# Masked keys for a cross attention's scores, values laid out for whole-row transfers, and a new order of work

## The reference

```
q, k, v = x @ Wq + bq, ctx @ Wk + bk, ctx @ Wv + bv        # 16 heads of 8
scores  = q . k / sqrt(8)
scores  = 0.5 * (scores * mask) + 0.5 * scores             # mask: 0 or 1
attn    = softmax(clip(scores, -50, 50))
y       = layernorm(x + (attn @ v) @ Wo + bo) * gamma + beta
```

```
q, k, v = rms_norm(y) @ to_qkv_w;  q, k = rope(q), rope(k)
keys    = [memory token x16, persistent x16, causal keys of the own segment]
x1      = y + softmax(q . keys / 8) @ values @ to_out_w
a, g    = rms_norm(x1) @ ff_w1 + ff_b1
out     = x1 + (silu(g) * a) @ ff_w2 + ff_b2
```

## Time and profile before

| | us |
|---|---|
| median of 3 runs | 1323.95 (1317.02 to 1329.44) |
| the profiled execution's own time | 1315.27 |
| its span, first to last instruction | 1313.5 |
| TensorE busy | 1155.9 (88%) |
| TensorE weight loads busy | 1001.2 (76%) |
| ScalarE busy | 1000.9 (76%) |
| GpSimd busy | 997.8 (76%) |
| VectorE busy | 954.3 (73%) |

### The profile page before, as it was taken

How to read it: one execution, slowest core, us unless ns; L and a number is a source line. 1 busy time by engine, 2 the same in 40 slices (tenths; PEclk the granted TensorE clock), 3 DMA queues, 4 the chain that set the end, 5 groups by cost and what they waited for, 6 DMA issues and landing times.

```text
span 1313.5 us, 53289 instructions
## 1 busy us (share of the span) xinstructions
PE 1155.9 (88%) x19811; PEld 1001.2 (76%) x19811; DVE 954.3 (73%) x2511; ACT 1000.9 (76%) x3149; POOL 997.8 (76%) x1678
## 2 busy tenths in 40 slices
PE   0569899999999999999999999999999999999986
PEld 0457788787788878787887878887787878887875
DVE  2446787778777877877787777778778777877772
ACT  1247788888888878788888887888888878888864
POOL 1246788888888888887888888788888888887874
PEclk9978999999999999999999999999999999999999
DMA  6322333333333333334333433333333333334321
GB/s 173 108 82 80 127 120 103 126 124 110 105 129 124 99 121 124 110 109 131 124 108 107 129 122 99 124 124 103 112 125 124 103 122 124 110 108 133 125 78 36
DMA packets 137337, 149.07 MB, mean 113 GB/s; under 512 B 14342, under 2 KB 119707, under 8 KB 137179
## 3 DMA queue, kind: packets, MB, share of 16 engines
q1 hardware_dynamic: 137306, 148.66, 35.6%
HBM read 40.11 MB, written 24.61 MB: 49 GB/s over the span
## 4 chain that ended last, share of the span: by engine, by line
DMA 36%; DVE 24%; PE 21%; SPq 11%; issue 6%; ACT 1%; POOL 1%; DVEq 0%; POOLq 0%; ACTq 0%
DMA qk_dram<-qk_parts 22%; DMA qk_stack<-qk_dram 11%; DVE ra L819 10%; DVE rb L819 10%; SPq L448 5%; SPq L440 5%; PE psum L990 5%; PE psum L1136 3%; PE psum L997 2%; PE psum L983 2%; DVE den L930 2%; PE psum L1017 1%; DMA maskT<-in 1%; PE psum L985 1%; PE psum L984 1%
## 5 line engine op out<-in xcount | busy, mean ns | idle before, releaser
L990 PE MATMUL psum<-xnT,wqkv 128*128 128x128 f32 x2048 | 252.0, 277 | 0.3 <-ACT memT L595 0.3
L990 PEld LDWEIGHTS psum<-xnT,wqkv 128*128 128x128 f32 x2048 | 241.1, 194 | 0.8 <-ACT memT L595 0.5
L516 POOL TENSOR_TENSOR probs_near<-probs,rden 128x256 f32<-128x256 f32 x256 | 158.5, 619 | 93.0 <-DVE rden L937 92.2
L824 DVE TENSOR_TENSOR z<-psum,wT 77x512 f32<-77x512 f32 x256 | 163.7, 679 | 46.6 <-PE psum L997 46.5
L506 POOL TENSOR_TENSOR qT<-ra,rs 128x512 f32<-128x512 f32 x128 | 163.4, 1276 | 34.9 <-DMA rs<-rb 34.9
L819 DVE TENSOR_TENSOR ra<-psum,rope 128x512 f32<-128x512 f32 x256 | 173.4, 677 | 15.0 <-PE psum L990 9.9
L819 DVE TENSOR_TENSOR rb<-psum,rope 128x512 f32<-128x512 f32 x256 | 173.9, 679 | 0.0
L508 POOL TENSOR_TENSOR kall<-ra,rs 128x512 f32<-128x512 f32 x128 | 163.0, 1274 | 5.2 <-DMA rs<-rb 5.2
L512 POOL TENSOR_SCALAR z<-z 77x512 f32<-77x512 f32 x256 | 151.0, 615 | 20.3 <-DVE z L824 19.8
L666 ACT ACTIVATE z<-z 77x512 f32<-77x512 f32 x256 | 148.6, 633 | 15.7 <-POOL z L512 15.5
L829 DVE TENSOR_REDUCE less_max<-psum 128x4 f32<-128x324 f32 x128 | 57.4, 490 | 141.7 <-PE psum L1012 141.7
(11 more groups left out here) (142 smaller groups left out, 3013.4 us busy)
## 6 DMA issues: line engine op xcount, KB each, us to landing
rs<-rb SPq DMA_DIRECT2D x256, 256.0 KB, 2.4
qk_dram<-qk_parts SPq DMA_DIRECT2D x64, 307.5 KB
qk_stack<-qk_dram SPq DMA_DIRECT2D x256, 76.9 KB
vals_far<-vals SPq DMA_DIRECT2D x128, 128.0 KB, 2.4
seq_in<-in SPq DMA_DIRECT2D x64, 166.5 KB
out<-out_sb SPq DMA_DIRECT2D x64, 64.0 KB, 1.8
maskT<-in SPq DMA_DIRECT2D x64, 38.5 KB
ctx_all<-in SPq DMA_DIRECT2D x5, 320.0 KB, 5.6
```

The lines of the kernel that those rows point to most:

```text
L516: nc.gpsimd.tensor_tensor(probs_near[:, slots, :], probs[:, slots, 0:SEG], scale.broadcast_to([S, 4, SEG]), ALU.mult)
L824: return V.tensor_tensor(z0[:, 4 * t:4 * t + 4, :], at(f"xs{t}")[0:S2, :].rearrange("k (h q) -> k h q", h=4), wT[:].unsqueeze(1).broadcast ...
L990: last = mm(at(name)[:, S * n:S * (n + 1)], wqkv[:, lo + 128 * n:lo + 128 * (n + 1)], xnT[:], start=n == 0)
```

## The change

- `qk_parts`, `qk_stack` and `qk_dram` go, with the float32r terms. VectorE writes `qb` (q with its bias) and `kz`: k with its bias four times, each copy multiplied by `own_rows`, a table of 0 and 1 that keeps one head's 8 rows in each group of 32 and zeroes the other 24. A cross score is then a plain float32 product of 32 rows against the four heads' queries in `qb`, in which only the own head's rows count. The host no longer permutes Wq and Wk. The copy of v into `v0` moves from ScalarE to VectorE.
- `less_maxima` and its cast identity go: all four tiles take the maximum as the bias of four exponentials each.
- The host permutes the value columns of `to_qkv_w`, so that `v0` holds all that the lower 64 partitions need from the upper ones, and `v1` the reverse. `vals_far` has one transfer of whole rows (2,048 bytes) behind each projection. `memv` is stored to DRAM in two transfers that undo the permutation.
- The mask comes with the input in one transfer, padded to 128 rows.
- Each engine's turn has a new order, and the banks a new table. `weigh` moves from the stage `seq[2]` to the end of `seq[3]`, `gate` from `seq[1]` to `seq[2]`, the pooled and memory tokens stay in the same turn. GpSimd's turn begins with the sum for q1; its sum for k1 ends the turn before. Its sum for q0 stands between `y_keep` and the power of L557; `xb` comes later. ScalarE's turn begins with the copies of the heads and ends with the mask of tile 3, the gate's six activations and the mask of tile 2.

```diff
-MEANS, POOLED, TOKENS_A, TOKENS_B = 3, 5, 2, 4
+MEANS, POOLED, TOKENS_A, TOKENS_B = 7, 7, 6, 3
 LEAD = 6
 QK = ("q0", "k0", "q1", "k1")
-SHIFTED_BY_PE = (2, 3)
...
-        seq_in = sb("seq_in", [128, S + S2 + D])
-        xT, ctxT, x_sb = seq_in[:, 0:S], seq_in[:, S:S + S2], seq_in[:, S + S2:]
-        maskT = sb("maskT", [S2, S])
+        seq_in = sb("seq_in", [128, S + S2 + D + S])
+        xT, ctxT, x_sb = seq_in[:, 0:S], seq_in[:, S:S + S2], seq_in[:, S + S2:S + S2 + D]
+        maskT = seq_in[0:S2, S + S2 + D:]
         wT = sb("wT", [S2, S])
         xb = sb("xb", [S, D])
-        qk_parts = sb("qk_parts", [D, 3, S + S2 + 1], F32R)
-        qk_stack = sb("qk_stack", [128, GROUP, S + S2 + 1], F32R)
+        qb = sb("qb", [D, S])
+        kz = sb("kz", [D, GROUP, S2])
...
             ("c0T", 0, 4, (c0T_ready,)),
+            ("wo", 3, 4, (y_ready,)),
+            ("out", 1, 2, (x1_ready,)),
+            ("v0", 0, 3, (vals0_ready,)),
+            ("xs0", 5, 5, (z0_masked,)),
+            ("xs1", 4, 5, (z1_masked,)),
+            ("xs2", 1, 5, (z2_masked,)),
+            ("xs3", 6, 5, (z3_masked,)),
+            ("scores0", 7, 3, (probs0_exp,)),
+            ("v1", 2, 3, (vals1_ready,)),
+            ("scores1", 0, 3, (probs1_exp,)),
+            ("xnT", 3, 4, (xnT_ready,)),
+            ("lin", 6, 1, (sT_ready,)),
+            ("hnT", 1, 2, (hnT_ready,)),
+            ("k1", 4, 4, (k1_rotated,)),
+            ("q1", 2, 4, (q1_rotated,)),
+            ("k0", 5, 4, (k0_rotated,)),
+            ("turned2", 0, 3, (probsT2_ready,)),
+            ("turned3", 3, 3, (probsT3_ready,)),
+            ("q0", 7, 4, (q0_rotated,)),
+            ("u", 4, 5, (u_kept,)),
             ("turned1", 1, 3, (probsT1_ready,)),
+            ("down", 6, 1, (out_ready,)),
+            ("turned0", 3, 3, (probsT0_ready,)),
+            ("gate", 2, 2, (gate_ready,)),
+            ("pv", 0, 5, (c0_ready,)),
+            ("scores3", 7, 4, (probs3_exp,)),
+            ("scores2", 5, 4, (probs2_exp,)),
+            ("o0", 6, 3, (oT0_ready,)),
+            ("o1", 4, 3, (oT1_ready,)),
+            ("o2", 1, 3, (oT2_ready,)),
+            ("o3", 3, 3, (oT3_ready,)),
+            ("qkv", 2, 6, (v0_kept,)),
...
+                for p in range(2):
+                    sp.dma_start(memv_dram.rearrange("b (c p e) -> b p c e", p=2, e=2 * DH)[:, p, :, :],
+                                 memv[:, BANK * p:BANK * (p + 1)].rearrange("b (c e) -> b c e", e=2 * DH)).then_inc(memv_stored, 16)
+                sp.wait_ge(memv_stored, 32)
 
             def body(n, seq, done):
-                if seq[2] is not None:
-                    if first(seq[2]):
-                        store_memory_values()
-                    sp.dma_start(vals_pre[0::BAND, :, :].rearrange("n (f h) d -> n f (h d)", f=2),
-                                 memv_dram[bass.ds(seq[2], 1), :].rearrange("b (f n e) -> (b n) f e", f=2, n=4)).then_inc(memv_in, 16)
-                if seq[3] is not None:
-                    sp.wait_ge(k1_rotated, done[4])
+                if seq[3] is not None:
+                    sp.wait_ge(k0_rotated, done[4])
                     passed(sp, sp_passed)
                     for odd in range(2):
-                        sp.dma_start(rs[odd::2, half(1)], rb[1 - odd::2, half(1)]).then_inc(swapped1_in, 16)
-                if seq[5] is not None:
-                    sp.wait_ge(k_rest_ready, done[6])
+                        sp.dma_start(rs[odd::2, half(0)], rb[1 - odd::2, half(0)]).then_inc(swapped0_in, 16)
+                    if first(seq[3]):
+                        store_memory_values()
+                    wait(sp, heads_filled, done[3])
                     passed(sp, sp_passed)
-                    sp.dma_start(qk_dram.rearrange("t p s -> p t s"), qk_parts[:, :, 0:S + S2].bitcast(F32)).then_inc(parts_out, 16)
-                    sp.wait_ge(parts_out, done[6] * 16)
-                    passed(sp, sp_passed)
-                    for r in range(GROUP):
-                        sp.dma_start(qk_stack[32 * r:32 * r + 3 * HD0, :, 0:S + S2].bitcast(F32),
-                                     qk_dram.rearrange("t (d r g) s -> r (t d) g s", r=GROUP, g=GROUP)[r]).then_inc(stacks_in, 16)
-                    if first(seq[5]):
-                        context_loads(2, 3)
-                        first_weights()
-                    if first(seq[4]):
-                        other_weights()
+                    sp.dma_start(vals_pre[0::BAND, :, :].rearrange("n (f h) d -> n f (h d)", f=2),
+                                 memv_dram[bass.ds(seq[3], 1), :].rearrange("b (f n e) -> (b n) f e", f=2, n=4)).then_inc(memv_in, 16)
                 if seq[0] is not None:
                     sp.wait_ge(out_ready, done[1])
                     passed(sp, sp_passed)
@@ -459,22 +442,28 @@
                 if seq[3] is not None:
                     sp.wait_ge(vals0_ready, done[4])
                     passed(sp, sp_passed)
-                    for p in range(2):
-                        sp.dma_start(vals_far[SEG * p:SEG * (p + 1), :, :],
-                                     vals[SEG * (1 - p):SEG * (2 - p), :].rearrange("k (a p e) -> k a p e", p=2, e=2 * DH)[:, :, p, :]).then_inc(vals_far_in, 16)
+                    sp.dma_start(vals_far[0:SEG, :, :].rearrange("k c e -> k (c e)"), vals[SEG:2 * SEG, 0:BANK]).then_inc(vals_far0_in, 16)
+                    sp.wait_ge(vals1_ready, done[4])
+                    passed(sp, sp_passed)
+                    sp.dma_start(vals_far[SEG:2 * SEG, :, :].rearrange("k c e -> k (c e)"), vals[0:SEG, BANK:2 * BANK]).then_inc(vals_far1_in, 16)
+                if seq[4] is not None:
+                    if first(seq[4]):
+                        other_weights()
+                    sp.wait_ge(q1_rotated, done[5])
+                    passed(sp, sp_passed)
+                    for odd in range(2):
+                        sp.dma_start(rs[odd::2, half(1)], rb[1 - odd::2, half(1)]).then_inc(swapped1_in, 16)
                 if seq[6] is not None:
+                    if first(seq[5]):
+                        context_loads(2, 3)
+                        first_weights()
+                    wait(sp, qkv_filled, done[6])
                     wait(sp, wT_ready, done[6])
                     wait(sp, xb_ready, done[6])
                     passed(sp, sp_passed)
                     sp.dma_start(seq_in[:], seq_pack[bass.ds(seq[6], 1), :, :].rearrange("b p n -> (b p) n")).then_inc(inputs_in, 16)
-                    sp.dma_start(maskT[:], mask_t[bass.ds(seq[6], 1), :, :].rearrange("b k s -> (b k) s")).then_inc(inputs_in, 16)
                     if first(seq[6]):
                         context_loads(0, 1)
-                if seq[4] is not None:
-                    sp.wait_ge(q0_rotated, done[5])
-                    passed(sp, sp_passed)
-                    for odd in range(2):
-                        sp.dma_start(rs[odd::2, half(0)], rb[1 - odd::2, half(0)]).then_inc(swapped0_in, 16)
 
             pipeline(sp, body)
...
-                if t in SHIFTED_BY_PE:
-                    return nc.scalar.activation(probs[:, 4 * t:4 * t + 4, :], heads(f"scores{t}"), ACT.Exp)
...
+            def keys_of_heads():
+                return V.scalar_tensor_tensor(out=kz[:], in0=at("qkv")[:, S:S + S2].unsqueeze(1).broadcast_to([D, GROUP, S2]),
+                                              scalar=cols[:, BK:BK + 1], in1=own_rows.unsqueeze(2).broadcast_to([D, GROUP, S2]),
+                                              op0=ALU.add, op1=ALU.mult)
...
+                    dve.wait_ge(qkv_filled, done[6])
+                    keys_of_heads()
+                    V.tensor_scalar(qb[:], at("qkv")[:, 0:S], cols[:, BQ:BQ + 1], None, ALU.add).then_inc(qb_ready, 1)
+                    V.tensor_copy(v0[:, :, 0:HD0], at("qkv")[0:S2, 256:384].rearrange("k (h d) -> k h d", h=H)).then_inc(v0_kept, 1)
...
             def cross_scores():
-                for g in range(GROUP):
+                for n in range(GROUP):
                     for r in range(GROUP):
-                        part = slice(32 * r, 32 * r + 3 * HD0)
-                        last = mm(at(f"xs{r}")[0:S2, S * g:S * (g + 1)], qk_stack[part, g, S:S + S2], qk_stack[part, g, 0:S])
+                        rows = slice(32 * r, 32 * (r + 1))
+                        last = mm(at(f"xs{r}")[0:S2, S * n:S * (n + 1)], kz[rows, n, :], qb[rows, :])
...
-            def less_maxima(t):
-                return mm(at(f"scores{t}")[:, 0:4 * KEYS].rearrange("i (n k) -> i n k", n=4), ident_b[:],
-                          less_max_b[:, 4 * t:4 * t + 4].unsqueeze(2).broadcast_to([S, 4, KEYS]), start=False)
...
-                                    head = 2 * (4 * f + n) + h
-                                    near = vals[keys, DH * head:DH * (head + 1)] if p == s else vals_far[keys, 2 * f + j, dims]
+                                    own = BANK * p + 2 * DH * (2 * f + j) + DH * h
```

(12 more changed lines are left out.)

561 lines of the change are left out of this document (253 added, 308 removed).

## The result

The changed kernel takes 1215.47 us (median of 4 runs, 1214.23 to 1217.26) against 1325.33 for the kernel before (median of 4, 1317.02 to 1329.44): a ratio of 0.918, 95% interval 0.913 to 0.923. The forecast was 1254, range 1220 to 1298. The direction was right, the gain of some 110 us is half as large again as the 70 forecast, and the time lies outside the range. There the kernel before had medians of 1318.58, 1317.31 and 1316.31 us, to which their ratios refer; the kernel after was not measured again, so a difference from its 1215.47 us is one between rounds.

What follows compares the result with a forecast made beforehand. TensorE's work plus its wait for the DRAM round trip bound the 19.08 us turn. Span 1313.5 - 47 (loop) - 15 (start) = 1251.5, 1253.3 with the 1.77 around it; forecast 1254 us, range 1220 to 1298.

Steps and rivals of the forecast that it cites:

- The stack wait: Loop: cross scores wait for the DRAM round trip's loads into the stacks; removing it saves 1.09 us a turn.
- TensorE's work: Loop: 17.67 us a turn plus 0.43 cross scores, minus 0.29 less_maxima, plus 0.16 shape changes: 17.97, between 17.67 and 18.41.
- I take both, 14.7: Start: TensorE's waits for the second input (11.62 us) and vals_pre (3.05) both go, -15 us.
- the lower bound of -25: Start: the largest gain allowed, -25 us, if the other two early DRAM trips count as well.
- The idle time that I kept: Loop: TensorE idle beyond the DRAM trip's wait stays at 0.32 us a turn, between 0.1 and 0.56.
- The late power: Loop: GpSimd's q0 sum delays the power that xn waits for by 0.24 us, with xn, its transpose and k1's projection.
- a new wait in place of the old: Rival, loop: late power, bank reuse and upper bounds make 18.9 us a turn, about 1290 us; chance 0.15.
- the upper bound: Cross scores, loop: 32 passes take 1.10 us, as those of L1003 do, +0.67 us a turn.
- The pass price of 27 ns: Cross scores, loop: 32 plain float32 passes at 27 ns each take 0.86 us, +0.43 a turn.
- my 0.08: TensorE's order, loop: each change of tile shape costs 0.08 us; two more a turn give +0.16.
- less_maxima's 0.29: TensorE, loop: dropping less_maxima saves 0.29 us a turn.
- deeper: Rival: float32 passes and shape changes at lower bounds, idle 0.1; 17.8 us a turn, start -20, about 1220 us; chance 0.10.

Runs made afterwards that it cites:

- the loads alone moved: Kernel before, with the loads of the context's second half and all weights issued ahead of the first wait for the DRAM trip: 1312.93 us, ratio 0.995.
- The masked keys alone: Kernel before with kz and qb replacing the DRAM round trip, start loads early too; orders, banks, less_maxima and mask transfer kept: 1295.01 us, ratio 0.983.
- with v1 ahead: Kernel after with v1 projected ahead of the cross scores, so that the two small-tile groups touch: 1235.21 us, ratio 0.938.
- with the input ahead: Kernel before with masked keys, input and mask in one transfer issued ahead of the two vals_far transfers: 1266.42 us, ratio 0.963.

## Why the prediction was wrong

**The bound was read rightly.** The stack wait of 1.09 us a turn went, TensorE took its place, its clock stayed at 1.00, and no other engine became the bound by its sum. Between the profiled spans the forecast was -62 us and the result -101.1. Of the 39.1 missing, 19 are in the 57 turns between the marks (13 idle time, 6 TensorE's work) and 20 in the start and the end together.

**The step that failed is the start**, "I take both, 14.7". It named two waits, 11.62 us for the second input and 3.05 for vals_pre; the start became 39.0 us shorter (my mark lay 25.6 us earlier, at 119.00, which makes up for 1 us of it). Two things were missed. First, the cause: the term counts the trip at the one row where TensorE waits for the second input behind it. The two later trips of the filling stand only in the lower bound of -25, at 10 us together, and not in the term. The chain of waits of the kernel before, up to the first output, has it three times:

```profile
15.47 4.52 DMA qk_dram<-qk_parts
...
73.05 4.50 DMA qk_dram<-qk_parts
...
79.36 2.23 DMA qk_stack<-qk_dram
...
119.00 4.45 DMA qk_dram<-qk_parts
...
124.72 2.35 DMA qk_stack<-qk_dram
```

From the store's start to the last landing the second takes 8.5 us and the third 8.1. Without the trip the start is 18.5 us shorter than with the loads alone moved, which gave 2.8. TensorE's clock is a part of the story too. The windows of the start, before and after:

```profile
60.00:80.00 20.00, 14.01 (x145) 9.59 (x143) 7.01 (x24) 8.72 (x26) 6.33 (x8) 0.72 0.22 77
80.00:100.00 20.00, 14.36 (x209) 11.77 (x212) 10.48 (x22) 8.34 (x22) 11.00 (x19) 0.76 0.37 115
100.00:120.00 20.00, 17.90 (x233) 15.39 (x237) 13.64 (x35) 14.46 (x47) 12.45 (x23) 0.85 0.30 94
```

```profile
60.00:80.00 20.00, 18.97 (x329) 16.28 (x329) 16.66 (x41) 16.20 (x56) 15.62 (x28) 1.00 0.27 87
80.00:100.00 20.00, 19.67 (x360) 17.20 (x362) 16.50 (x44) 17.54 (x60) 16.68 (x29) 1.00 0.25 86
100.00:120.00 20.00, 20.00 (x356) 17.75 (x345) 17.37 (x46) 17.29 (x56) 16.91 (x31) 1.00 0.31 104
```

Before, after waits and little work, the granted clock was 0.72 to 0.85 there, a mixture of its two levels, 1.2 and 2.4 GHz; TensorE was busy 85.0 us up to the first output, against 77.8 after. The row with 0.89 for the whole start was in my own group and I drew nothing from it. Taking the trip away does not by itself bring the clock back. The masked keys alone have between 60 and 80 us:

```profile
60.00:80.00 20.00, 16.55 (x189) 12.99 (x183) 14.11 (x34) 10.68 (x32) 9.32 (x20) 0.71 0.21 59
```

Second, the order: I gave it the load order and the store of the memory values alone, the second at 3.05 us, where it has 6.0 on the kernel's own chain (from the store at 90.89 to `weigh` at 96.90). VectorE's totals stood in plain sight, and moved they are 7.2 us. The rest of the change is 10.5, which I have only as a remainder: that store is in it, and so is `weigh`, which now follows in the same turn as its scores. How much of each of these shares is clock is open.

**The idle time that I kept** was the second term mis-sized: 0.32 us a turn forecast, 0.10 measured, 0.22 x 57 = 13 us. The late power was argued rightly and costs nothing: xn waits for it 7.6/39 = 0.2 us a turn, as the table of waits says, but TensorE has scores(0) to do before the transpose of `xn`, and `lin` after it. I had priced a wait of ScalarE as one of TensorE. The rival "a new wait in place of the old" would have been right about the old order, where the masked keys alone brought 0.25 us a turn of new waiting. In the new one no such wait is left.

**TensorE's work**, 17.97 forecast, is 17.86, and that this is so near is luck: errors cancel. The masked cross scores cost 1.05 - 0.43 = 0.62, near the upper bound, not 0.43. The pass price of 27 ns was right to the digit (0.87 for 32); the rest is 0.18 us in the group. Ahead of it 0.25 us are lost, of which the change of shape is 0.10, near my 0.08, and 0.15 have no proven cause. The Trainium skill's sentence in TensorEngine Tiling (Array Packing), Key Properties, that a change of tiling mode drains TensorE, agrees with the traces as far as there is a cost: 0.10 us ahead of the 64-row tiles and, with v1 ahead, of the 32-row ones (0.33 instead of 0.23 between starts), and 0.18 more in the group. Against that, busy time fell elsewhere: 18.34 us a turn in the old order with masked keys, 18.05 with the input ahead, with the same products. Most of that stands around the one wait that went. With the masked keys alone the last product ahead of qkv (L1010, 611.52) is counted busy for 0.27 us and qkv's first row (L1156, 612.01) takes 0.33 until the next. With the input ahead the same product is followed after 0.11, and that row takes 0.22. So in this turn 0.27 of the 0.29 us are the edges of a wait, counted as work. How much of that kind was in the 17.67 that my sum started from, around the stack wait, no run shows. less_maxima's 0.29 was 0.1 in the old order; in the new one it was not measured alone.

**Parts that I gave nothing** were worth nothing where they were measured: that is the values' layout, in the new order. The padding of the mask was not measured alone. The packed load was worth 28.6 us in the old order together with the input's place in SyncE's queue, and which of the two it was is not separated; I had it as a clause in the idle time.

**Of the rivals**, "deeper" comes nearest in time (about 1220), but only half of its mechanism came true. The idle time of 0.1 us a turn did; the passes at their lower bound did not, and the turn is 17.96 us, not 17.8. That the total still fell below it is the start, 39.0 us where it had 20. All my bounds for the start had the same flaw: they were made of waits seen in TensorE's rows, whereas the start is one chain through all engines, and shortening it moves everything behind it. The range should have reached down to what the start would be if TensorE were as busy in it as in the new loop.

## What to carry to other kernels

When a wait is to be taken away, read what stands behind it in the same queue: here the removal took 1.09 us of waiting a turn away and brought 0.25 of another back, part of which went only when the input was moved ahead of vals_far. And set against the wait the work that replaces it, 0.62 us. Cost the filling of a pipeline as a chain through all engines, not by TensorE's idle rows, and look at the granted clock in it. A wait of an engine that is not the bound is not a term of the sum, however plainly a reordering lengthens it.

## What was not expected of the hardware

The first 32 passes of 32-row tiles after full-size products cost 1.05 us, the next 32 in the same shape 0.87. They start 0.10 late with v1 ahead and 0.25 late in the kernel after. So a visit to the shape costs 0.28 to 0.43 us, as much as 10 to 16 passes, and the upper 0.15 of it may have another cause.

TensorE's busy time for the same products differed by 0.29 us a turn (18.34 and 18.05) between two kernels that differ in SyncE's transfers alone: the edges of a wait are counted as busy.
